# Attention's q and k loads with their rows numbered (part, d, repeat), and quad 2's load issued behind the first two shifts

## The chip, the cores and the metric

The kernel runs on one core of a Trainium2 chip. The metric is the device time of one execution in microseconds, the median of several runs. A core has five engines with a queue each: TensorE (PE, matrix products), VectorE (DVE), ScalarE (ACT), GpSimd (POOL) and SyncE (SP, which here only waits and issues DMAs), and sixteen DMA engines that all queues share.

## The reference

A block of four stages over x of shape (2, 1024, 128), each on the layer norm of x and added to it: a gated convolution mix, a feed-forward stage, attention and the feed-forward stage again. The change is in the attention, of 16 heads with 8 dimensions each:

```
qkv = x @ qkv_w.T + qkv_b
qkv = qkv.reshape(B, S, H, 3 * hd)            # B 2, S 1024, H 16, hd 8
qkv = jnp.transpose(qkv, (2, 0, 3, 1))
q, k, v = jnp.split(qkv, 3, axis=2)
scores = jnp.einsum('hbds,hbdt->hbst', q, k) / jnp.sqrt(jnp.float32(hd))
w = jax.nn.softmax(scores, axis=-1)
attn = jnp.einsum('hbst,hbdt->hbsd', w, v)
```

## The kernel before

All values of the first two stages stay in SBUF. For attention, q and k are made in four chunks of 512 tokens (NCH 4, two for each batch) for all heads at once. Each is split into three bfloat16 parts whose sum is the float32 value (PARTS 3). `store_parts(c)` (L308 to L314) writes the parts of chunk c to the DRAM tensors q_scr and k_scr, six DMAs of 128 KB for a chunk. The stored layout is (part, g and d, chunk, j, token), and the stores' access pattern has j (4) outermost.

Attention then runs over eight quads, each four heads of one batch (n = 0 to 7; b = n // 4). A quad's q and k come back from DRAM by `load_quad(n)` (L316 to L327), six DMAs: for each i of the three parts one for q and one for k. Each fills 24 rows (partitions) of the tile qt or kt with 8 KB apiece, 192 KB. Since the product of two sums of three parts has nine terms, and d has 8 values, a score is a sum over 72 rows (QK_ROWS): the rows of qt hold q's part i three times, those of kt all three parts of k against it. Three buffers for each of qt and kt take the quads in turn (NBUF 3; the third buffer lies in the memory of val, and so the trace calls it val).

Three further rows hold the shift: the negated maximum of each row of scores, in three bfloat16 parts, against rows of ones in kt. The exponent's argument thus comes out of one product over 96 rows (L1294). The maximum comes from products of its own over 72 rows (L1229), each of which VectorE reduces (L895). After the 32 units of half a quad, `turn_max` (L1236) turns the maxima, VectorE negates them (L908), GpSimd splits them into nm_s (L446 to L452), and SyncE writes them into qt by `load_shift(hn)` (L329 to L336), three DMAs of 4 KB that wait for shift_split.

TensorE's order in attention: it waits for quad 0's loads, runs 32 units of maxima for half 0 of quad 0 and 16 of half 1 (LEAD), and waits for shift 0 before the first exponent product. Then each step (16 a quad) has four exponent products (e), four maxima ahead of time (m) and the product of the previous step's exponentials with v (v), by ORDER "emememevm" (L57). The maxima of the next quad begin at step 4, with a wait for its loads (qk_in, L1308). ScalarE computes the exponentials (L648).

SyncE's order around the change stands in L338 to L361: ones into kt, the parts of chunks 0 and 1, a wait for both, load_quad(0), the parts of chunks 2 and 3, load_quad(1) and load_quad(2), load_shift(0). In the loop over n then load_quad(n + 2) for n from 1, after a wait for the exponent products that read the buffer, load_shift(2n + 1) and load_shift(2n + 2). A DMA that waits holds up all issues behind it on this queue.

Of the kernel before, what the change touches and what calls it, by code (L numbers as in the profile page):

```python
# [21 lines left out]
B, L, D = 2, 1024, 128  # L22
# [15 lines left out]
H, HD = 16, 8  # L38
QH = 4
GQ = H // QH  # L40
NQ = B * GQ
PARTS = 3
# [3 lines left out]
NBUF = 3  # L46
# [65 lines left out]
def build(nc, ins, out):  # L112
# [3 lines left out]
    with ctx:  # L116
        def sb(name, shape, dt=F32):
            return ctx.enter_context(nc.sbuf_tensor(name, shape, dt))

        def sem(name):  # L120
            return ctx.enter_context(nc.semaphore(name))
# [54 lines left out]
        h = sb("h", [P, NT, D])  # L176
# [51 lines left out]
        k_scr = nc.dram_tensor("k_scr", [PARTS, GQ * HD, NCH, QH, CH], BF16, kind="Internal").ap()  # L228
# [28 lines left out]
        qk_in = [sem(f"qk_in{r}") for r in range(NBUF)]  # L257
# [19 lines left out]
        @block.sync  # L277
        def _(sp):
            for c in range(NCH):
                sp.dma_start(x[:, TC * c:TC * c + TC, :], x_src[:, TC * c:TC * c + TC, :]).then_inc(s_x[c], 16)  # L280
            for at, v in vectors[5:]:
                sp.dma_start(vec_n[at:at + v.shape[0], :], v).then_inc(s_vec, 16)
            for at, v in q_k_biases:
                sp.dma_start(vec_n[at:at + 1, :].rearrange("a (h d) -> a h d", d=HD), v).then_inc(s_vec, 16)
            for dst, src in ((ksym[:, :, :], sym_k.rearrange("(k p) o t -> p k (o t)", p=P)),
                             (a_n[:, :, :], A_d.rearrange("(k p) s -> p k s", p=P)),
                             (kdwa[:, :, :], dwa_k.rearrange("(k p) o t -> p k (o t)", p=P))):
                sp.dma_start(dst, src).then_inc(s_w_taps, 16)
            sp.dma_start(wfc_n[:, :, :], wfc_d.rearrange("(m p) d -> p m d", p=P)).then_inc(s_w_tern, 16)
            sp.dma_start(wpr_n[:, :], wproj_d).then_inc(s_w_tern, 16)  # L290
            for dst, src in ((pw_n[:, :, :], pw_w.rearrange("(k p) c -> p k c", p=P)), (hb_n[:, :], hb_w),
                             (ha_n[:, :], ha_w), (fu_n[:, :, :], fuse_w.rearrange("(k p) c -> p k c", p=P)),
                             (ow_n[:, :], out_w), (bm_n[:, :], Bm_d)):
                sp.dma_start(dst, src).then_inc(s_w_mix, 16)
            sp.dma_start(u_n[:, :, :], u_d.rearrange("(m p) r -> p m r", p=P)).then_inc(s_w_ffn, 16)
            sp.dma_start(v_n[:, :], v_d).then_inc(s_w_ffn, 16)
            sp.dma_start(fb_n[:, :], fb_d).then_inc(s_w_ffn, 16)
            sp.dma_start(gate_n[:, :], gate_d.broadcast_to([RANK, 1])).then_inc(s_w_ffn, 16)

            sp.wait_ge(pads_ready, 5)  # L300
            for b in range(B):
                sp.wait_ge(u_read, 2 * (b + 1))
                for t in range(DC):
                    at = PAD + 1 - t
                    sp.dma_start(us[32 * t:32 * t + 32, b, at:at + L],
                                 u_rows[32 * t:32 * t + 32, b, :]).then_inc(us_in[b], 16)

            def store_parts(c):  # L308

                for w, scr in ((0, q_scr), (1, k_scr)):  # L310
                    sp.wait_ge(split_ready, 2 * c + w + 1)
                    for i in range(PARTS):
                        sp.dma_start(scr[i, :, c, :, :].rearrange("x j t -> j x t"),
                                     qk_s[c % 2][:, w, i, :]).then_inc(scr_done[c % 2], 16)  # L314

            def load_quad(n):  # L316
                b, g = divmod(n, GQ)
                rows = slice(g * HD, (g + 1) * HD)
                for i in range(PARTS):

                    at = i * PARTS * HD
                    src = q_scr[i, rows, 2 * b:2 * b + 2, :, :].rearrange("d h j t -> d (h j t)")
                    dst = qt[n % NBUF][at:at + PARTS * HD, :, :, :].rearrange("x h j t -> x (h j t)")
                    sp.dma_start(dst, src.unsqueeze(0).broadcast_to([PARTS, HD, QH * L])).then_inc(qk_in[n % NBUF], 16)
                    src = k_scr[:, rows, 2 * b:2 * b + 2, :, :].rearrange("i d h j t -> i d (h j t)")
                    dst = kt[n % NBUF][at:at + PARTS * HD, :, :, :].rearrange("x h j t -> x (h j t)")
                    sp.dma_start(dst, src).then_inc(qk_in[n % NBUF], 16)  # L327

            def load_shift(hn):  # L329

                sp.wait_ge(shift_split, hn + 1)
                n, half = divmod(hn, 2)
                for i in range(PARTS):
                    dst = qt[n % NBUF][SHIFT_ROW + i:SHIFT_ROW + i + 1, half, :, :]
                    sp.dma_start(dst.rearrange("a j (k p) -> a (j k) p", p=P),
                                 nm_s[:, i, :]).then_inc(shift_in, 16)  # L336

            sp.wait_ge(consts_ready, 2 * NBUF + 1)  # L338
            for r in range(NBUF):
                sp.dma_start(kt[r][SHIFT_ROW:SHIFT_ROW + PARTS, :, :, :].rearrange("i h j t -> i (h j t)"),  # L340
                             ones_rows).then_inc(qk_in[r], 16)
            store_parts(0)
            store_parts(1)
            for i in range(2):
                sp.wait_ge(scr_done[i], STORED)
            load_quad(0)
            store_parts(2)
            store_parts(3)
            for n in range(1, NBUF):
                load_quad(n)  # L350
            load_shift(0)
            for n in range(NQ):
                if 1 <= n and n + 2 < NQ:
                    sp.wait_ge(exp_mm, STEPS * QH * n)
                    if n + 2 == GQ:
                        for i in range(2):
                            sp.wait_ge(scr_done[i], 2 * STORED)
                    load_quad(n + 2)
                load_shift(2 * n + 1)
                if n + 1 < NQ:  # L360
                    load_shift(2 * n + 2)  # L361
            for c in range(NCH):
                sp.wait_ge(tok_read, TOK_F2[c] + 1)
                sp.dma_start(out_dst[:, TC * c:TC * c + TC, :], x[:, TC * c:TC * c + TC, :]).then_inc(stored, 16)
            sp.wait_ge(stored, 16 * NCH)
# [1009 lines left out]
```

## Time and profile before

| | us |
|---|---|
| median of 3 runs | 629.66 |
| lowest, highest | 626.11, 629.94 |
| span of the profiled execution | 623.5 |
| TensorE busy | 546.7 (88%) |
| VectorE busy | 480.4 (77%) |
| ScalarE busy | 349.4 (56%) |
| GpSimd busy | 113.0 (18%) |

The profile is of one execution. Times are from the start of its span, which is shorter than the measured time of a run. The page's chain follows the work that ended last back from the end, at each step to what released it. PE is TensorE's products and PEld its weight loads. A line such as L1229 is one of the kernel, out<-in are tiles. Idle time of an engine that is not the bottleneck costs nothing. What the DMA queues moved:

```profile
DMA packets 14664, 18.95 MB, mean 30 GB/s; under 512 B 3801, under 2 KB 12936, under 8 KB 13448
q1 hardware_dynamic: 13818, 17.54, 8.2%
```

### The profile page before, as it was taken

Reading aid. Unit: us, or ns where it says so; the run is one execution under the profiler, and the core shown is the slowest. Engines: PE = TensorE matmul, PEld = TensorE weight load, DVE = VectorE, ACT = ScalarE, POOL = GpSimd, SP = SyncE. Lnnn points to the kernel's source line nnn. Section 1 sums busy time; section 2 is a strip of 40 time slices with the busy share of each in tenths; the row PEclk is TensorE's granted clock in tenths of the full one; section 3 lists DMA queues with packets and bytes.
Section 4 is the critical chain, followed back from the end, with each engine's and each line's share of the span. In section 5 each row is a group of like instructions: output and inputs, shape, how many; then the busy total and the mean of one; then the engine's idle time right before and its main releaser. Section 6 shows DMA issues by size and latency. Waiting matters only on the chain.

```text
span 623.5 us, 9634 instructions
## 1 busy us (share of the span) xinstructions
PE 546.7 (88%) x2831; PEld 218.8 (35%) x2831; DVE 480.4 (77%) x965; ACT 349.4 (56%) x667; POOL 113.0 (18%) x155
## 2 busy tenths in 40 slices
PE   2986899872591699999999999899999999999887
PEld 2443656561110133333333333233333333323366
DVE  6999579971593388888898898788888888863473
ACT  2764314433000377777777677677777777778551
POOL 6947708334000000100100100100100000000000
PEclk9997899887555599999999999999999999999999
DMA  8030000021221000010010010010010000000001
GB/s 205 8 69 0 2 1 1 5 82 74 87 85 81 25 1 2 27 52 2 29 51 2 29 51 2 32 51 2 19 61 2 2 2 1 1 2 1 1 18 52
DMA packets 14664, 18.95 MB, mean 30 GB/s; under 512 B 3801, under 2 KB 12936, under 8 KB 13448
## 3 DMA queue, kind: packets, MB, share of 16 engines
q1 hardware_dynamic: 13818, 17.54, 8.2%
q0 software_dynamic: 240, 0.46, 0.7%
q8 instruction: 28, 0.46, 0.3%
q10 hardware_dynamic: 550, 0.27, 0.1%
q14 instruction: 28, 0.22, 0.1%
HBM read 12.75 MB, written 4.19 MB: 27 GB/s over the span
## 4 chain that ended last, share of the span: by engine, by line
PE 69%; DVE 16%; DMA 8%; ACT 3%; issue 2%; SPq 2%; POOL 0%; ACTq 0%; DVEq 0%
PE ps L1256 20%; PE ps L1229 18%; PE ps L1294 17%; PE ps L1034 5%; PE ps L1044 5%; DVE mx L895 3%; DMA qt<-nm_s 3%; DVE acc L794 3%; DMA kt<-k_scr 2%; DVE h L710 2%; DVE acc L840 1%; DMA k_scr<-gate 1%; PE ps L1243 1%; ACT gate L648 1%; DVE st L687 1%
## 5 line engine op out<-in xcount | busy, mean ns | idle before, releaser
L895 DVE TENSOR_REDUCE mx<-ps 128x1 f32<-128x512 f32 x512 | 319.5, 681 | 70.8 <-PE ps L1229 70.8
L648 ACT ACTIVATE gate<-ps 128x512 f32<-128x512 f32 x256 | 134.3, 604 | 112.2 <-PE ps L1294 112.2
L1229 PE MATMUL ps<-kt,qt 72*128 72x512 bf16 x384 | 157.7, 417 | 18.0 <-DMA kt<-k_scr 18.0
L1294 PE MATMUL ps<-qt,kt 96*128 96x512 bf16 x384 | 143.0, 386 | 21.6 <-DMA qt<-nm_s 18.2
L648 ACT ACTIVATE acc<-ps 128x512 f32<-128x512 f32 x256 | 132.3, 602 | 49.8 <-PE ps L1294 49.8
L1229 PEld LDWEIGHTS ps<-kt,qt 72*128 72x128 bf16 x384 | 38.3, 100 | 131.9 <-DVE mx L895 81.0
L1256 PE MATMUL ps<-gate,v 128*32 128x512 f32 x512 | 69.3, 611 | 0.7 <-ACT o_sb L639 0.7
L1256 PE MATMUL ps<-acc,v 128*32 128x512 f32 x512 | 68.2, 605 | 0.6 <-ACT acc L648 0.6
L446 POOL CAST nm_s<-nm 16x128 bf16<-16x128 f32 x16 | 4.6, 287 | 331.4 <-DVE nm L908 331.4
L1294 PEld LDWEIGHTS ps<-qt,kt 96*128 96x128 bf16 x384 | 37.5, 99 | 65.0 <-DMA qt<-nm_s 18.8
L1229 PE MATMUL ps<-val 72*128 72x512 bf16 x128 | 48.8, 382 | 0.0
L1294 PE MATMUL ps<-val 96*128 96x512 bf16 x128 | 48.6, 380 | 0.0
L794 DVE SCALAR_TENSOR_TENSOR acc<-val,ksym,acc 128x512 f32<-128x512 f32 (+1 forms) x40 | 38.4, 1033 | 0.0
L1044 PEld LDWEIGHTS ps<-wp_T,acc 128*128 128x128 f32 x256 | 29.5, 192 | 2.4 <-issue 1.9
L1034 PE MATMUL ps<-hT,fc_T 128*128 128x512 f32 x64 | 30.3, 618 | 0.0
L1044 PE MATMUL ps<-wp_T,acc 128*128 128x128 f32 x256 | 29.7, 275 | 0.0
L405 POOL TENSOR_TENSOR acc<-acc,attn 128x512 f32<-128x512 f32 x8 | 27.2, 3404 | 13.7 <-ACT attn L523 12.6
L602 ACT ACTIVATE gate<-ps 128x512 f32<-128x512 f32 x32 | 18.2, 596 | 17.6 <-DVE acc L840 10.7
L1229 PEld LDWEIGHTS ps<-val 72*128 72x128 bf16 x128 | 12.5, 98 | 34.6 <-DVE mx L895 23.5
L840 DVE TENSOR_TENSOR acc<-gate 128x512 f32<-128x512 f32 x32 | 21.5, 719 | 3.0 <-ACT gate L602 3.0
L1256 PEld LDWEIGHTS ps<-gate,v 128*32 128x32 f32 x512 | 10.6, 108 | 27.8 <-ACT acc L648 11.8
L1256 PEld LDWEIGHTS ps<-acc,v 128*32 128x32 f32 x512 | 10.1, 108 | 27.9 <-ACT acc L648 14.6
(181 smaller groups left out, 473.3 us busy)
## 6 DMA issues: line engine op xcount, KB each, us to landing
qt<-q_scr SPq DMA_DIRECT2D x18, 192.0 KB
kt<-k_scr SPq DMA_DIRECT2D x18, 192.0 KB
val<-q_scr SPq DMA_DIRECT2D x6, 192.0 KB
val<-k_scr SPq DMA_DIRECT2D x6, 192.0 KB
x<-in_L_attn_a_x SPq DMA_DIRECT2D x4, 256.0 KB, 4.5
us<-h SPq DMA_DIRECT2D x8, 128.0 KB, 2.4
out<-x SPq DMA_DIRECT2D x4, 256.0 KB, 2.2
q_scr<-attn SPq DMA_DIRECT2D x6, 128.0 KB
```

What stands on the lines that cost most here:

```text
L405: pool.tensor_tensor(dst, dst, tap_buf(j), ALU.add).then_inc(tap_added, 1)
L602: act.activation(relu[:, n % NR, :], bank(2 + i % 4), ACT.Relu).then_inc(wide_read, 1)
L648: act.activation(pexp[s % NPB][:, j, :], bank(exp_bank(n0, s * QH + j, last)[0]), ACT.Exp, scale=SCALE).then_inc(exp_done, 1)
L710: ins = dve.tensor_scalar(h[:, i, :], x[:, i, :], small[:, f, 2, i:i + 1], small[:, f, 3, i:i + 1], ALU.mult, ALU.add)
L794: ins = dve.scalar_tensor_tensor(out=dst, in0=src, scalar=ksym[:, k, j:j + 1], in1=dst, op0=ALU.mult, op1=ALU.add)
L840: dve.tensor_tensor(r2_buf[:, c % 2, m, :], r, r, ALU.mult).then_inc(sq_ready, 1)
L895: dve.tensor_reduce(mx[:, half, u // 2, u % 2:u % 2 + 1], bank(MBANKS[k % 4]), AX.X, ALU.max).then_inc(m_read, 1)
L1034: mm = pe.matmul(bank(2 + i % 4), w, a, start=(k == 0), stop=(k == len(pairs) - 1))
L1044: mm = pe.matmul(bank(6 + i % 2)[:, t * P:(t + 1) * P], a, w, start=(k == 0), stop=(k == len(group) - 1))
L1229: pe.matmul(bank(MBANKS[k % 4]), qt[r][0:QK_ROWS, half, j, c * P:(c + 1) * P], kt[r][0:QK_ROWS, keys, j, :], start=True, stop=True).then_i ...
L1256: mm = pe.matmul(bank(2)[VW * j:VW * (j + 1), :], v4[r][:, s % BT, j, :], pexp[s % NPB][:, j, :], start=(s % BT == 0), stop=(s % BT == BT ...
L1294: pe.matmul(bank(at_bank), keys, qt[r][:, half, j, :], start=True, stop=True).then_inc(exp_mm, 1)
```

## The change

In load_quad the repeat dimension of q's source moves from outermost to second, and so does the part dimension of k's source. Row 3d + r of a group of 24 rows holds what row 8r + d held before; q and k change alike. The destination, the 24 rows and the bytes are as they were. In SyncE's order load_quad(2) moves from ahead of load_shift(0) to behind load_shift(1).

```diff
@@ load_quad
-                    sp.dma_start(dst, src.unsqueeze(0).broadcast_to([PARTS, HD, QH * L])).then_inc(qk_in[n % NBUF], 16)
-                    src = k_scr[:, rows, 2 * b:2 * b + 2, :, :].rearrange("i d h j t -> i d (h j t)")
+                    sp.dma_start(dst, src.unsqueeze(1).broadcast_to([HD, PARTS, QH * L])).then_inc(qk_in[n % NBUF], 16)
+                    src = k_scr[:, rows, 2 * b:2 * b + 2, :, :].rearrange("i d h j t -> d i (h j t)")
                     dst = kt[n % NBUF][at:at + PARTS * HD, :, :, :].rearrange("x h j t -> x (h j t)")
                     sp.dma_start(dst, src).then_inc(qk_in[n % NBUF], 16)
@@ SyncE's order
             store_parts(3)
-            for n in range(1, NBUF):
-                load_quad(n)
+            load_quad(1)
             load_shift(0)
             for n in range(NQ):
                 if 1 <= n and n + 2 < NQ:
...
                     load_quad(n + 2)
                 load_shift(2 * n + 1)
+                if n == 0:
+                    load_quad(2)
                 if n + 1 < NQ:
                     load_shift(2 * n + 2)
```

## Rows read from the trace of the kernel before

**Rows 1.** The page: clock row of 40 slices, chain by engine and line, two groups.

```profile
PEclk9997899887555599999999999999999999999999
...
PE 69%; DVE 16%; DMA 8%; ACT 3%; issue 2%; SPq 2%; POOL 0%; ACTq 0%; DVEq 0%
PE ps L1256 20%; PE ps L1229 18%; PE ps L1294 17%; PE ps L1034 5%; PE ps L1044 5%; DVE mx L895 3%; DMA qt<-nm_s 3%; DVE acc L794 3%; DMA kt<-k_scr 2%; DVE h L710 2%; DVE acc L840 1%; DMA k_scr<-gate 1%; PE ps L1243 1%; ACT gate L648 1%; DVE st L687 1%
...
L1229 PE MATMUL ps<-kt,qt 72*128 72x512 bf16 x384 | 157.7, 417 | 18.0 <-DMA kt<-k_scr 18.0
L1294 PE MATMUL ps<-qt,kt 96*128 96x512 bf16 x384 | 143.0, 386 | 21.6 <-DMA qt<-nm_s 18.2
```

**Rows 2.** Chain of waits, 136 to 209 us: start us, us, what.

```profile
136.23 7.83 DMA k_scr<-gate
...
147.81 14.23 DMA kt<-k_scr
...
162.80 19.82 DVE mx L895 x33
...
187.59 20.74 DMA qt<-nm_s
```

**Rows 3.** Timeline of TensorE, 188 to 209 us: start us, us, what, idle time before.

```profile
187.74 2.40 PE L1229 MATMUL ps<-kt,qt 72*128 72x512 bf16 x4
208.38 0.61 PE L1294 MATMUL ps<-qt,kt 96*128 96x512 bf16 x1 [18.25 <-DMA qt<-nm_s]
```

**Rows 4.** Windows: stretch, length, busy us PE, PEld, DVE, ACT, POOL, PEclk, DMA, GB/s.

```profile
4.00:6.00 2.00, 0.00 (x0) 0.00 (x0) 1.50 (x8) 0.44 (x1) 2.00 (x4) 1.00 1.15 356
136.00:144.00 8.00, 7.31 (x28) 4.71 (x26) 2.88 (x6) 3.01 (x5) 2.14 (x2) 0.79 0.26 91
190.00:200.00 10.00, 0.14 (x1) 0.00 (x0) 1.86 (x4) 0.00 (x0) 0.00 (x0) 0.50 0.19 81
192.00:208.00 16.00, 0.00 (x0) 0.00 (x0) 0.00 (x0) 0.00 (x0) 0.00 (x0) 0.50 0.18 76
209.00:218.00 9.00, 9.00 (x25) 2.45 (x24) 5.44 (x8) 4.94 (x9) 0.00 (x0) 0.50 0.01 2
218.00:220.00 2.00, 2.00 (x10) 0.66 (x12) 1.78 (x4) 1.74 (x4) 0.00 (x0) 0.82 0.00 0
```

**Rows 5.** The tile nm_s, its sixteen shifts: from issue to landing.

```profile
DMA to landing us min/median/max: 1.7/1.8/20.7
```

**Rows 6.** Timeline of SyncE's queue: start us, us, line, operation, out<-in, count.

```profile
144.12 0.76 SPq L324 DMA_DIRECT2D qt<-q_scr  x1
...
148.53 9.87 SPq L313 DMA_DIRECT2D q_scr<-attn  x3
...
182.26 2.09 SPq L327 DMA_DIRECT2D val<-k_scr  x1
185.81 2.37 SPq L335 DMA_DIRECT2D qt<-nm_s  x3
228.55 1.77 SPq L335 DMA_DIRECT2D qt<-nm_s  x3
252.05 1.77 SPq L335 DMA_DIRECT2D qt<-nm_s  x3
```

**Rows 7.** Timelines of TensorE and VectorE ahead of the first maxima.

```profile
143.14 1.05 PE L1044 MATMUL ps<-att_T,hT 128*128 128x128 f32 x8
146.19 0.68 DVE L859 TENSOR_TENSOR us<-ps,bv_bc 128x512 f32<-128x512 f32 x1
```

**Rows 8.** Timeline of TensorE: quad 1's first maximum, and two turned maxima.

```profile
223.84 0.38 PE L1229 MATMUL ps<-kt,qt 72*128 72x512 bf16 x1
226.24 0.28 PE L1236 MATMUL ps<-ident,mx_row 128*16 128x128 f32 x1
249.74 0.28 PE L1236 MATMUL ps<-ident,mx_row 128*16 128x128 f32 x1
```

## The prediction

> **What bounds the kernel now.** I read the page first. TensorE is busy for 88% of the span, and the chain that ended last is 69% TensorE, yet 8% of it is transfers: qt<-nm_s 3%, kt<-k_scr 2%, k_scr<-gate 1% [rows 1]. The diff only touches transfers, so the question is where one of them holds up the program.
>
> The chain of waits between 136 and 209 us answers it [rows 2]. SyncE waits for the stores of the q and k parts until 144.06. Then it issues the six loads of quad 0, and the last lands 14.23 us after its issue, at 162.04. The row maxima follow on VectorE, 33 reductions in 19.82 us, then the merged row maxima are turned and negated, and GpSimd splits the first shift into three parts (nm_s). SyncE issues them from 185.81 [rows 6], and the last takes 20.74 us to land. TensorE, which has done its last early maximum at 190.14, starts the exponent products at 208.38 after 18.25 us of idle time [rows 3]. The reader is to see that this chain has only two transfers that could be shorter, and no compute engine works beside either: between 192 and 208 us every engine shows 0.00 busy [rows 4].
>
> Is either a matter of latency? The other landings of the shift say no: the median of all is 1.8 us, the longest 20.7 [rows 5]. So the 20.74 us are queueing. The issues on SyncE's queue show behind what [rows 6]: six loads of quad 0, twelve stores (parts of chunks 2 and 3), six loads of quad 1, six of quad 2, and then the shift. The windows give the rates [rows 4]. With loads alone (190 to 200 us) 81 GB/s move at a DMA share of 0.19, and 0.19 x 16 = 3.0 engines: 27 GB/s for each. With stores alone (136 to 144) it is 91 GB/s at 0.26, that is 4.2 engines. In the code the loads' source has an outermost dimension of 3 (the repeats for q, the parts for k), and the stores' source has one of 4 (j). A transfer thus runs on as many engines as its outermost dimension counts, here.
>
> Do these rates explain the times? A quad is 6 x 192 KB = 1,180 kB, at 81 GB/s 14.6 us. From first issue (144.12) to landing (162.04) are 17.9 us, so 3.4 us are issue and latency. The twelve stores are 12 x 128 KB = 1,573 kB, at 91 GB/s 17.3 us. From 162.0: 17.3 + 14.6 + 14.6 gives 208.5, and the shift landed at 187.59 + 20.74 = 208.33. The queue is understood to 0.2 us.
>
> **The change, part by part.** *Rows numbered with d outermost.* Each load keeps its 24 rows of 8 KB and its bytes; the sums over rows don't depend on their order, and q and k get the same one. The outermost dimension of the source goes from 3 to 8, which divides the destination's 24 rows too. By the reading above the load then runs on 8 engines. No row shows a transfer on eight, so I bound its rate from the two sides: 8 x 27 = 216 GB/s if each engine keeps what it has on three, and 8 x 22 = 178 GB/s if each falls to what sixteen give (356 GB/s at 4 to 6 us, /16 = 22) [rows 4]. A quad takes 5.5 or 6.6 us; I take 6.0, between the two, since eight lies between three and sixteen. Issue doesn't limit it: six loads go out in 0.72 us each [rows 6], 4.4 us. Quad 0 lands 14.6 - 6.0 = 8.6 us earlier, at 153.4. Below nothing isn't possible unless engines get fewer (a rival).
>
> Who else would hold TensorE then? Its last earlier product ends at 144.2, VectorE's last v tile at 146.9 [rows 7]. Both lie ahead of 153.4, so the maxima start 8.6 us earlier, and the whole train behind them too: the shift is ready at 177.2, issued to 179.6 (185.81 + 2.37 - 8.6), TensorE out of early maxima at 181.5.
>
> The Trainium skill has a rule against the full gain. "SBUF — State Buffer", section "Door 1: The DMA port swizzle", says that a transfer's rate depends on how many of 16 ports its partitions reach, some 27.2 GB/s each, four neighbouring partitions to a port. A 24-row load reaches 6, so by an estimate from that page 163 GB/s and 7.2 us for a quad: a gain of 7.4 us at this place instead of 8.6, and a total 1.2 us higher. No row of before can decide it, because three engines stay below six ports.
>
> *Quad 2's load behind the first two shifts.* Six issues (4.3 us of SyncE's time) and 14.6 us of queue (6.0 at the new rate) leave the place ahead of load_shift(0). Ahead of the shift now: quad 0 done by about 151.6 (landing less latency), stores 17.3 us to 168.9, quad 1 6.0 us to 174.9 on the engines that both use. That is 2.3 us before the shift is issued at 177.2. The shift then takes its usual 1.8 us after the last issue: 187.59 - 8.6 + 1.8 = 180.8, still 0.7 us before TensorE is free for it (181.5). The stall of 18.25 us becomes about nothing. If the queue needs longer, the first 3.0 us cost nothing and each further one a whole us.
>
> What is late next? Quad 2's load now waits for shift 1, which is issued at 228.55 [rows 6], in the new time 26.8 us earlier: 201.8, landing by about 212 with the new rate. Its first use is the maxima of quad 2, from step 4 of quad 1. Half a quad is 23.5 us (the turned maxima at 226.24 and 249.74), and quad 1's first maximum is at 223.84, so quad 2's is at 223.84 + 47.0 = 270.8, in the new time 244.0 [rows 8]: 32 us of cover. Queued behind the moved issues is load_shift(2), whose issue at 252.05 follows POOL's split, not the queue [rows 6]; it becomes 225, long after the six issues. GpSimd's queue isn't passed.
>
> *Later quads.* Five more loads of six transfers get shorter, but TensorE waits for transfers only at two places in the stretch, and the page shows 18.0 us for the one form and 18.2 of the other in the whole run, which are these [rows 1, 3]. Worth nothing; their cover is the exponent work of the quad before.
>
> *TensorE's clock.* It was granted half speed, 1.2 GHz, from 156 us on (the fives of the clock row, slices 11 to 14 of 15.6 us) [rows 1], in the maxima and in the stall, and went back to 2.4 GHz about 10 us after the exponent products began (0.50 at 209 to 218, 0.82 in 218 to 220) [rows 4]. I shift this stretch as it is. If the maxima ahead without an idle gap brought the rise forward, up to 5 us more would come back (about 10 us at half speed); if it came later by the same chance, 1 or 2 us would be lost. The maxima, though, ran 28 us at 0.50 with no rise, so I take nothing.
>
> **Sum.** Profiled execution: 623.5 - 8.6 - 18.2 = 596.7. The runs' median is 629.66, 6.2 above the span; the difference applies there too: 602.8. The three runs reach from 626.11 to 629.94, so the measure is good to about 2 us, and half a per cent, and 1% (6 us) is about what can be told from no change.
>
> **Rivals.**
> (a) *The rate stays.* If not the outer dimension but the 24 rows set the number of engines (24 rows are three times 8), the loads stay at 81 GB/s. For it: 3 fits 24/8. Against it: stores with 128 rows ran at 4.2 engines, which 128/8 = 16 doesn't give. Then only the move counts: the shift lands behind quad 1, 14.6 us earlier, TensorE starts at 193.8: 629.7 - 14.6 = 615.1.
> (b) *The shift still waits.* Stores and loads meet on engines 0 to 3 and stores slow down, or loads keep to 178 GB/s or the ports' rate. For it: only 3.0 us of slack. With 3 to 6 us lost: 606 to 609.
> (c) *The clock rises sooner*: 598 to 601, with the price above.
> (d) *Slower.* The new order puts a load on fewer engines. It decides from two engines down: at 54 GB/s a quad takes 21.8 us, and 144.1 + 3.4 + 21.8 + 17.3 + 21.8 = 208.4, the shift's landing of today. On one engine (27 GB/s) a quad takes 43.7 us: the shift lands at about 252, and the time is 673. Against it: both shapes seen so far ran on as many engines as they had outermost rows, and there are more now.
> The rule of the Trainium skill in "DMA: Bandwidth & Descriptors", section "Why a DMA increments its semaphore by 16 and not by 1", is that the engines are the largest number up to 16 that divides both outermost sizes; it gives 8 for 8 and 24, against (a) and (d), and the trace's 3 and 4 agree with it.
>
> **Chances.** The forecast (600 to 606) 0.72; (a) 0.09; (b) 0.11; (c) 0.06; (d) 0.02. The likeliest is the number: 602.8. The range takes the forecast, (b) and most of (c): 598.5 to 609. Faster by over 1% hold all but (d): 0.97. Within 1%: 0.01. Slower: 0.02.
>
> **What would show it.** The DMA share during quad 0's load near 0.5 instead of 0.2, and its rate near 200 GB/s; TensorE's wait for kt<-k_scr 9 us instead of 18.0; maxima starting at 153 to 155; the landing of the first shift under 3 us, with TensorE's wait for it gone; quad 2's issues at about 202 and no new wait at quad 1's step 4. I am wrong if the share stays at 0.19, if the shift still takes over 5 us to land, or if the clock's rise moves by more than 3 us against the first exponent product.

## The result, and the profile after

The changed kernel takes 601.62 us (median; 601.03 to 602.98) against 629.8 (626.11 to 630.09) for the kernel before: a ratio of 0.9588, interval 0.956 to 0.9616. The span of its profiled execution is 599.0 us, before 623.5.

First the chain of waits of the changed kernel, in the same stretch as [rows 2] (start us, us, what):

```profile
144.64 0.69 SPq L324
...
148.14 6.94 DMA kt<-k_scr
...
155.22 0.60 PE ps L1230
...
155.84 19.82 DVE mx L896 x33
...
176.19 6.96 PE ps L1230 x13
183.15 0.43 PE ps L1295
```

The six loads of quad 0 land 6.94 us after the last issue instead of 14.23. From there VectorE's 33 reductions take 19.82 us, as before. Then the chain stays on TensorE: the step "DMA qt<-nm_s", 20.74 us in [rows 2], isn't there. TensorE's timeline says the same against [rows 3], and so does the tile nm_s against [rows 5]:

```profile
175.98 7.16 PE L1230 MATMUL ps<-kt,qt 72*128 72x512 bf16 x13
182.94 0.63 PE L1295 MATMUL ps<-qt,kt 96*128 96x512 bf16 x1
```

```profile
DMA to landing us min/median/max: 1.7/1.8/2.8
```

The first exponent product carries no idle time; it starts at 182.94 instead of 208.38. The longest landing of any shift is 2.8 us, where it was 20.7; the first shift lands in 1.8. The page's groups put what is left of the waits for transfers at one place, against 18.0 and 18.2 in [rows 1]:

```profile
L1230 PE MATMUL ps<-kt,qt 72*128 72x512 bf16 x384 | 157.7, 417 | 10.6 <-DMA kt<-k_scr 10.6
L1295 PE MATMUL ps<-qt,kt 96*128 96x512 bf16 x384 | 143.1, 387 | 3.2 <-issue 2.0
```

Windows of the changed kernel (stretch, length, busy us of PE, PEld, DVE, ACT, POOL, granted clock, DMA share, GB/s), against [rows 4]:

```profile
147.00:151.00 4.00, 0.00 (x0) 0.00 (x0) 0.39 (x1) 1.74 (x2) 3.16 (x5) 0.60 0.53 172
176.00:178.00 2.00, 2.00 (x6) 0.42 (x4) 2.00 (x5) 0.00 (x0) 0.70 (x2) 0.50 0.22 78
178.00:180.00 2.00, 2.00 (x5) 0.31 (x3) 2.00 (x4) 0.00 (x0) 0.69 (x2) 0.50 0.11 41
374.00:382.00 8.00, 7.23 (x32) 1.84 (x33) 3.63 (x7) 4.62 (x9) 0.40 (x1) 0.79 0.41 134
```

During quad 0's load the DMA share is 0.53, that of eight engines and a little, and 172 GB/s move: 21.5 for each engine, where three engines had 27. Quad 1 is through only between 178 and 180 us, about when the shift is issued (178.82).

**Where 24.5 us of span come from.** The first exponent product starts 25.4 us earlier. The granted clock rose 9.2 us after it instead of 10.2, which gives half a us more. So the turned maximum of quad 0's second half is at 200.25 instead of 226.24, 26.0 earlier, and the distance stays until 343 us of the kernel before. At one turn of the loop over quads TensorE idles for 2 us in both kernels (1.98 at 374.77, before 2.07 at 400.85). In the profile of before the clock held behind it (1.00 from 400 to 408 us); in the changed kernel's it falls once, to about half speed from 376 to 380 us (0.62 and 0.53 in its two halves; 0.79 in the last window above). That costs 1.45 us: the turned maximum at 438.90 before is at 414.36, 24.5 earlier, and so is the end.

### The profile page after: what moved, and what is told of

Its sections match the earlier page's. It is cut to its first block, busy times and chain, and to the rows that moved or that the text cites. A ratio compares the mean times of both kernels' runs of the same rounds, so it can differ in the third digit from the quotient of the medians.

```text
span 599.0 us, 9634 instructions
## 1 busy us (share of the span) xinstructions
PE 548.1 (92%) x2831; PEld 218.8 (37%) x2831; DVE 479.6 (80%) x965; ACT 349.2 (58%) x667; POOL 112.2 (19%) x155
## 4 chain that ended last, share of the span: by engine, by line
PE 73%; DVE 17%; DMA 3%; ACT 3%; issue 2%; SPq 1%; POOL 0%; ACTq 0%; DVEq 0%
PE ps L1257 21%; PE ps L1230 20%; PE ps L1295 18%; PE ps L1035 6%; PE ps L1045 5%; DVE acc L795 3%; DVE mx L896 3%; DVE h L711 2%; DMA k_scr<-gate 1%; DVE acc L841 1%; PE ps L1244 1%; ACT gate L649 1%; DMA kt<-k_scr 1%; DVE st L688 1%; ACT acc L649 1%
## 5 line engine op out<-in xcount | busy, mean ns | idle before, releaser
L1230 PE MATMUL ps<-kt,qt 72*128 72x512 bf16 x384 | 157.7, 417 | 10.6 <-DMA kt<-k_scr 10.6
L603 ACT ACTIVATE gate<-ps 128x512 f32<-128x512 f32 x32 | 18.2, 597 | 17.6 <-DVE acc L841 10.7
L841 DVE TENSOR_TENSOR acc<-gate 128x512 f32<-128x512 f32 x32 | 21.5, 718 | 3.0 <-ACT gate L603 3.0
L1257 PEld LDWEIGHTS ps<-gate,v 128*32 128x32 f32 x512 | 10.5, 108 | 27.6 <-ACT acc L649 11.8
L1257 PEld LDWEIGHTS ps<-acc,v 128*32 128x32 f32 x512 | 10.1, 108 | 27.9 <-ACT acc L649 14.6
```

The source lines that it names most:

```text
L603: act.activation(relu[:, n % NR, :], bank(2 + i % 4), ACT.Relu).then_inc(wide_read, 1)
L841: dve.tensor_tensor(r2_buf[:, c % 2, m, :], r, r, ALU.mult).then_inc(sq_ready, 1)
L1230: pe.matmul(bank(MBANKS[k % 4]), qt[r][0:QK_ROWS, half, j, c * P:(c + 1) * P], kt[r][0:QK_ROWS, keys, j, :], start=True, stop=True).then_i ...
L1257: mm = pe.matmul(bank(2)[VW * j:VW * (j + 1), :], v4[r][:, s % BT, j, :], pexp[s % NPB][:, j, :], start=(s % BT == 0), stop=(s % BT == BT ...
```

## The experiments

All are variants of the two kernels. Only where said do stored layouts differ; all compute the reference's output in full. The diffs are excerpts against the changed kernel, without their indentation; "..." stands for what is left out, and where a quad has more than six loads, the semaphore counts grow with them. Several profiles issue quad 0's first load up to 1.3 us later than the changed kernel's (144.64), so times are compared from that issue where it matters.

**The move alone (order_only).** The row order is that of the kernel before:

```diff
-sp.dma_start(dst, src.unsqueeze(1).broadcast_to([HD, PARTS, QH * L]))...
-src = k_scr[:, rows, 2 * b:2 * b + 2, :, :].rearrange("i d h j t -> d i (h j t)")
+sp.dma_start(dst, src.unsqueeze(0).broadcast_to([PARTS, HD, QH * L]))...
+src = k_scr[:, rows, 2 * b:2 * b + 2, :, :].rearrange("i d h j t -> i d (h j t)")
```

> Only the move: quad 2's loads behind the first two shifts, the rows as in the kernel before. Theory (a transfer runs on as many DMA engines as its outermost dimension counts, so the two parts of the change act through one queue): quad 0 lands as before at 162, the shift stands behind the stores and quad 1 only, so it lands 14.6 us earlier, at 193.8, and TensorE's idle time before the first exponent product is 18.25 - 14.5 = 3.7 us. About 615 us, 14.5 below the kernel before. Rival (the gain comes from the new row order alone): 629 to 630.

613.09 us (ratio 0.9758, 0.9723 to 0.9792, beside runs of before at 627.62). TensorE waits 3.5 us for the shift, where 3.7 were expected, and 14.5 us are gone, as the theory had it.

**The row order alone (rows_only).** Quad 2's loads are back ahead of load_shift(0).

> Only the new row order; quad 2's loads stay ahead of the first shift. Theory: quad 0 lands at 155 as in the changed kernel. The queue ahead of the shift is then quad 0, stores 17.3, quads 1 and 2 at 7.1 each: quad 1 is through at about 177, quad 2 at 184, and the shift lands at 184 to 186 while TensorE is free for it at 183. So 1 to 3 us of the stall stay, and the run takes 603 to 605: with the faster loads the move is worth only 1 to 3 us. Rival (the move carries most of the gain whatever the rate is): the shift still stands behind a whole quad's loads and 14 us are missing, 612 or more.

610.81 us (0.973, 0.9685 to 0.9774). Between the two expectations, and nearer to the rival. Its chain:

```profile
149.05 7.17 DMA kt<-k_scr
...
181.23 11.39 DMA qt<-nm_s
...
192.67 0.61 PE ps L1294
```

Quad 0 lands 7.17 us after its last issue, nearly as in the changed kernel, but the shift lands at 192.6, not at 184 to 186, and TensorE waits 8.4 us. The windows show what was missing from my sum:

```profile
168.00:172.00 4.00, 4.00 (x7) 0.62 (x6) 4.00 (x8) 0.00 (x0) 0.00 (x0) 0.50 0.53 172
172.00:184.00 12.00, 11.33 (x22) 2.10 (x21) 12.00 (x23) 0.00 (x0) 1.40 (x4) 0.50 0.51 109
```

The share is that of eight engines in both. By the rate in [rows 4] the stores keep four engines busy until about 172 (154.4 + 17.3), while the other four have begun with quad 1 (issued from 165.88). From 172 us all eight carry loads, but they move 109 GB/s, where quad 0's loads on eight engines had 172 in the changed kernel. The first four are then behind the others: the two halves work at different loads. The changed kernel has a shorter such stretch (115 GB/s at a share of 0.48 from 172 to 174 us). Whether this is the cause is taken up with st16_q2first.

**Fewer engines (eng4, eng2).** Each load is cut into two of 4 values of d, or four of 2. A quad's rows, bytes and order are those of the changed kernel; the outermost dimension falls, each DMA fills 12 or 6 rows instead of 24, and the issues grow:

```diff
+for d0 in range(0, HD, 4):                 # eng2: 2
+    rows = slice(g * HD + d0, g * HD + d0 + 4)
+    part = slice(at + PARTS * d0, at + PARTS * (d0 + 4))
-    dst = qt[n % NBUF][at:at + PARTS * HD, :, :, :]...
+    dst = qt[n % NBUF][part, :, :, :]...
```

> The changed kernel with each load cut into two of 4 values of d (12 rows): outermost dimension 4, same rows, same bytes, same row order, twice the issues. Theory (the outermost dimension sets the engines): four engines at 24 to 27 GB/s, 96 to 108 GB/s; a quad takes 11 to 12.3 us instead of 7.1, the first maximum starts at 159 to 160.5; quad 1 is through at 144.6 + 1.6 + 11.6 + 17.3 + 11.6 = 186.7, the shift lands at about 188 where TensorE is free at 187.5; 606 to 608 us. Rival (24 rows, or the row order as such, give the rate): 601.6 plus at most 1 us for the issues.

> The same cut into four of 2 values of d (6 rows): outermost dimension 2. Theory: two engines at 27 GB/s, 54 GB/s, a quad takes 21.8 us. The first maximum starts at about 169, the shift lands at about 208.4: the time of the kernel before, 628 to 631, although quad 2's loads are out of the way. Rival (24 rows, or the row order as such, give the rate): 602 to 604.

eng4: 608.78 us (0.9715, 0.9688 to 0.9742). eng2: 660.2 us (1.0545, 1.0499 to 1.0592, beside 626.97). First eng4's window, then eng2's, during quad 0's loads:

```profile
147.00:159.00 12.00, 0.00 (x0) 0.00 (x0) 0.57 (x1) 1.91 (x2) 3.29 (x5) 0.56 0.25 90
```

```profile
147.00:160.00 13.00, 0.00 (x0) 0.00 (x0) 0.93 (x2) 2.25 (x3) 3.28 (x5) 0.50 0.13 47
```

And two waits of eng2's whole span (us in total, times, the longest):

```profile
PE ps L1298 <- DMA qt<-nm_s: 20.6, 5, 11.9
...
PE ps L1298 <- DMA val<-nm_s: 10.5, 2, 5.5
```

Shares of 0.25 and 0.13 are 4 and 2 engines. That fewer rows in a DMA did it is ruled out by the other kernels: the same 24 rows had three engines before and have eight in the changed kernel, and 8 rows have eight in sp1 below. The rival falls.

eng4 came out slightly above its 606 to 608: at 90 GB/s instead of 96 to 108 the first maximum starts at 161.06, and TensorE waits 2.1 us for the shift. For eng2 I had the shift, and so the first exponent product, at about 208.4; it starts at 211.91, after 11.85 us of idle time, 3.5 later. The rest of the 33 us that it is slower than the kernel before comes afterwards: TensorE waits seven times for a shift, 31.1 us together, and only the longest is the first shift's. The six others follow the loads of quads 2 to 7. In the kernel before, a quad's loads in the loop are issued 18.0 us ahead of a shift:

```profile
257.49 0.73 SPq L324 DMA_DIRECT2D qt<-q_scr  x1
...
275.50 1.82 SPq L335 DMA_DIRECT2D qt<-nm_s  x3
```

From first issue to landing a quad takes 17.9 us on three engines: just fast enough. On two, quad 0's maxima start 26.9 us after the first issue. The six waits in the loop are 19.2 us; some 11 more stand beside a lower clock (eng2's mean over the span is 0.907, against 0.926 in base, the kernel before measured again, and 0.945 in the changed kernel), and I haven't split them.

**k's loads on twelve engines (k12).** k_scr is stored as (g d, part, chunk, j, token), and the 24 rows are one dimension:

```diff
-src = k_scr[:, rows, 2 * b:2 * b + 2, :, :].rearrange("i d h j t -> d i (h j t)")
+src = k_scr[rows, :, 2 * b:2 * b + 2, :, :].rearrange("d i h j t -> (d i) (h j t)")
...
```

> The changed kernel, with k_scr stored as (g d, part, chunk, j, token), so that the 24 rows of a k load are one dimension of 24 and divide by 12. q's loads stay at 8. Theory E (each DMA engine has about 21 us-GB/s in these loads, 167/8 GB/s, whatever rows it writes): k's loads run on 12 engines and take 0.79 us instead of 1.18, a quad 1.2 us less, the first maximum at about 154.0 instead of 155.2, 600.4 us. Theory P (the 24 rows themselves limit a transfer to some 165 GB/s): a quad takes 7.1 us as now, 601.6 us. If 8 is the limit of engines for another reason: 601.6 as well, with a DMA share of 0.5 during the loads.

603.22 us (0.9622, 0.9569 to 0.9676), no gain; from the first issue to the first maximum its profile has 11.7 us instead of 10.6. Its window in quad 0's loads:

```profile
149.00:156.00 7.00, 0.00 (x0) 0.00 (x0) 0.00 (x0) 0.78 (x1) 2.19 (x5) 0.54 0.59 123
```

More engines are busy (0.59, that of 9.4 engines) and less is moved (123 GB/s, 13 for each). Theory E is out: an engine has no rate of its own of 21 GB/s. That it got slower neither theory had. q's loads run on eight engines and k's on twelve here, so again engines may get out of step; that this is the reason isn't shown.

**Neighbouring or spread rows (sp1, sp3).** This pair changes only which rows one DMA writes. Both cut each load into three of 8 rows, 8 engines, 64 KB. They differ only in the rows that one DMA fills:

```diff
+for a in range(PARTS):
+    part = slice(at + HD * a, at + HD * (a + 1))              # sp1: 8 neighbours
+    part = slice(at + a, at + PARTS * HD, PARTS)              # sp3: every third of 24
+    src = q_scr[i, rows, 2 * b:2 * b + 2, :, :].rearrange("d h j t -> d (h j t)")
+    dst = qt[n % NBUF][part, :, :, :].rearrange("x h j t -> x (h j t)")
+    sp.dma_start(dst, src).then_inc(qk_in[n % NBUF], 16)     # and k_scr[a, rows, ...] into kt
```

> The changed kernel with each load cut into three, one for each repeat or part: 8 rows of 8 KB, 8 engines, rows numbered as in the changed kernel, so the 8 rows of a DMA lie three apart and spread over all 24. 18 DMAs a quad instead of 6. Theory E (each engine has its own rate of some 21 GB/s with eight at work) and theory P (what limits is how many groups of four neighbouring rows a transfer writes at a time; 24 rows touch six) expect the same here: the data take 7.1 us, the 18 issues at 0.6 us take 10.8, so the issues set it, the first maximum comes 13 to 14 us after the first issue, 604 to 605 us.

> The same 18 DMAs with 8 rows of 8 KB on 8 engines, but rows numbered as in the kernel before (the repeat outermost): the 8 rows of a DMA are neighbours. Theory E: as sp3, 604 to 605 us. Theory P: eight neighbours are two groups of four, and two groups give what two engines gave (53 GB/s, 26.5 each); a quad takes about 22 us, the first maximum comes 25 us after the first issue, and the loop's loads delay its shifts too: 640 to 660 us.

> The changed kernel once more, unchanged, beside the three kernels below on one chip: 601 to 603 us, with the first maximum 10.6 us after the first issue of quad 0's loads, as before.

after2 (the changed kernel again): 601.51 us, from first issue to first maximum 10.5 us (144.56 to 155.02). sp3: 605.33 us (0.9615, 0.9563 to 0.9666), 13.7 us (145.07 to 158.80). sp1: 618.59 us (0.9824, 0.9777 to 0.9871), 19.0 us (145.96 to 164.99). A window of sp3, then one of sp1, in quad 0's loads:

```profile
149.00:156.00 7.00, 0.00 (x0) 0.00 (x0) 0.00 (x0) 0.19 (x1) 1.59 (x4) 0.50 0.34 104
```

```profile
149.00:160.00 11.00, 0.00 (x0) 0.00 (x0) 0.00 (x0) 1.12 (x1) 2.77 (x5) 0.56 0.52 69
```

And the first issue on SyncE's queue in each, sp3 first, then sp1:

```profile
145.07 0.65 SPq L326 DMA_DIRECT2D qt<-q_scr  x1
```

```profile
145.96 0.29 SPq L326 DMA_DIRECT2D qt<-q_scr  x1
```

sp3 is held by its issues, as expected: its share is 0.34, between one and the next the engines have nothing to do. sp1 has eight engines busy all the time (0.52) and moves 69 GB/s, 8.6 for each. Same number of engines, same pieces, same sources: which rows are written decides. So for 8 neighbouring rows the rows set what eight engines give, not the engines. The Trainium skill, "SBUF — State Buffer", section "Door 1: The DMA port swizzle", gives 27.2 GB/s for each port that a transfer reaches, four neighbouring rows to a port. By an estimate from that page 8 neighbours get 54 GB/s and 24 rows 163. The runs' 69 and 172 lie above both, by 28% and 5%; that DMAs behind one another reach other ports is a possible reason that no run shows.

sp1's time was in neither theory's range. 19.0 - 3.4 = 15.6 us a quad instead of 22, and the loop's shifts bear that as they did the 14.6 of before: only the first one is waited for, 1.8 us. Some 5 us more are lost at the turn of the loop where TensorE idles for 2 us: the ninth and tenth of the sixteen turned maxima lie 32.5 us apart, instead of 27.3 in the changed kernel. The granted clock is 0.50 there from 394 to 400 us, while the changed kernel has some 4 us at half speed; why it is longer is open.

**Stores on sixteen engines (st16), and with quad 2 in front (st16_q2first).** The DRAM tensors have j and (g d) as neighbours, q three times over:

```diff
-sp.dma_start(scr[i, :, c, :, :].rearrange("x j t -> j x t"), qk_s[c % 2][:, w, i, :])...
+# q_scr [PARTS, NCH, QH, GQ * HD, PARTS, CH], the part broadcast over the repeats
+dst = scr[i, c, :, :, :, :].rearrange("j x a t -> (j x) a t")
...
+# k_scr [NCH, QH, GQ * HD, PARTS, CH]
+dst = scr[c, :, :, i, :].rearrange("j x t -> (j x) t")
...
+src = q_scr[i, 2 * b:2 * b + 2, :, rows, :, :].rearrange("h j d a t -> (d a) (h j) t")
+src = k_scr[2 * b:2 * b + 2, :, rows, :, :].rearrange("h j d i t -> (d i) (h j) t")
```

> The changed kernel with both DRAM tensors laid out so that the stores' 128 rows (j, g d) are one dimension: the stores run on 16 engines instead of 4. q is stored three times over (its repeats are in DRAM), so its loads' 24 rows are one dimension too; the loads' pieces are 1 KB instead of 8. Theory: the stores of chunk 1, 8 us from the last issue to landing now, land within 3 to 4 us; quad 0 lands at about 149, 6 us earlier; the first maximum starts there, since VectorE's v tile is ready at 147; 595 to 596 us. Rival (pieces of 1 KB, or three times the q bytes, eat the gain): loads take 3 us or more longer, 599 to 603.

> The kernel st16 (stores on 16 engines, loads on 12) with quad 2's loads back ahead of the first two shifts. In rows_only the eight engines of the loads ran at 107 to 115 GB/s together, with engines 0 to 3 held by the stores and 4 to 7 ahead of them. Theory: with the stores on all engines no engine runs ahead, quads 1 and 2 load at 155 to 160 GB/s and are through by about 172, before the shift is issued at 174; no stall, within 1 us of st16 (596). Rival (two quads of loads ahead of the shift always hold it up once they are shorter than 24 rows allow): a stall of 5 us or more, 601 or more.

st16: 595.98 us (0.9482, 0.9447 to 0.9517), as expected, though the first maximum starts at 150.74 and not at 149. st16_q2first: 595.33 us (0.946, 0.9414 to 0.9507). TensorE's timeline of the second, from the first maximum to the first exponent product:

```profile
148.51 19.91 PE L1234 MATMUL ps<-kt,qt 72*128 72x512 bf16 x35 [5.31 <-DMA kt<-k_scr]
...
169.27 7.20 PE L1234 MATMUL ps<-kt,qt 72*128 72x512 bf16 x13
176.26 0.63 PE L1299 MATMUL ps<-qt,kt 96*128 96x512 bf16 x1
```

Its windows, first with the stores, then with the loads of quads 1 and 2:

```profile
148.00:152.00 4.00, 3.49 (x8) 0.85 (x8) 2.87 (x5) 0.00 (x0) 0.00 (x0) 0.54 1.08 378
...
156.00:168.00 12.00, 12.00 (x21) 2.08 (x20) 12.00 (x21) 0.00 (x0) 0.00 (x0) 0.50 0.83 169
```

The stores move at 378 GB/s. The loads of quads 1 and 2 together run at 169 GB/s through 12 us, where rows_only had 109, and no exponent product waits, though quad 2 stands ahead of the shift. So the move is worth nothing here. Two things carry that. The stores are through sooner, and the loads of quads 1 and 2 are issued from 151.59 instead of 165.88. And the slow stretch is gone, as it has to be if it comes from engines out of step. How much each carries isn't split. This kernel's loads also run on twelve engines, in pieces of 1 KB, so the stores aren't the only thing that changed, and what slows the two halves in rows_only isn't shown. By an estimate from the same section of the Trainium skill, halves that stand one group of 24 rows apart reach four or five ports together, 109 or 136 GB/s, but halves two groups apart reach six; which of these rows_only had, its trace doesn't show.

The run shows one more thing: twelve engines move hardly more into 24 rows than the 172 GB/s of eight. It is 169 GB/s here, at a share of 0.83 (twelve sixteenths are 0.75, and the sixteen engines of the stores show 1.08), and 179 from 140 to 144 us, in quad 0's loads. From eight engines on, more of them bring little there, with the piece size as another difference.

**The kernel before once more (base).**

> The kernel before once more, unchanged, for a second profile. The profiled execution of before had a span of 623.5, which is 6.2 below its runs' median; that of the changed kernel lies 2.0 below its own run (599.0 and 601.03). If the profiled execution of before was one of the short ones (626.11), a second one has a span near 627.5, and the extra 4 us stand in one place of the trace. If not, spans of 623.5 come with runs of 629.7.

Span 624.6 us in a run of 626.68; its ten runs have a median of 627.61 (625.13 to 633.42). So the first of the two expectations holds in its first half: run less span is 2.1 here, about 2 as in all kernels of this study, and the profiled execution of before was a short one. The second half doesn't: 624.6 isn't 627.5. Its clock row also has a fall at the 26th slice, as the changed kernel's has:

```profile
PEclk9997899886555599999999999899999999999999
```

It costs the same here as there: from the ninth to the tenth turned maximum this profile takes 27.4 us, the changed kernel's 27.3, and the first profile of before 25.8. All other profiles of this study take 27.2 or more, so it was the first profile of before that was out of line. The rest of the spread between runs of the kernel before, some 4 us, isn't explained.

## Why the prediction was right, and where its numbers weren't

**The two stalls.** Right. Both terms acted where they were placed. The move alone gives 14.5 us, by the queue that was read from the trace and as rival (a) put it. The rows alone leave 8.4 us of the stall, more than the same queue gives, since it had no term for engines out of step.

**Eight engines.** Right: the share is 0.53, and with eng4 and eng2 the outermost dimension is shown as the cause. One reading was wrong in its wording: the 4 (j) of the stores is the outermost dimension of their DRAM destination, and their source has 128 rows. So the smaller of the two sides counted there, which the rule of the two sides that the prediction quotes covers and "the source's outermost dimension" doesn't. Rivals (a) and (d) are out for the change itself. But (d)'s point of balance was mis-sized: it counted only the first shift. At two engines the kernel is 33 us slower, since the loop's shifts wait too. "Worth nothing; their cover is the exponent work of the quad before" held for more engines, but was silent on the shift behind each quad's loads.

**The rate.** The term that was mis-sized. I took 6.0 us for a quad, from rates of three and sixteen engines. From first issue to landing are 10.4 us instead of 17.9: 7.5 gained, not 8.6, so a quad takes 7.1 us, outside both of my bounds (5.5 and 6.6), and the first maximum starts at 155.22, just past the 153 to 155 that I had named. The estimate from the Trainium skill's page was 7.2. The step that failed is that the rate of eight engines lies between those of three and sixteen: neither row said which rows were written. sp1 shows that the rows can set the rate at eight engines, and st16_q2first that 24 rows take hardly more from twelve (169 and 179 GB/s). The miss itself is small, though: 21.5 GB/s for each engine against 22 at sixteen. That the rows, and not the engines, hold the changed kernel at 172 fits these two runs but isn't shown by itself.

**The queue ahead of the shift.** The sum had quad 1 through at 174.9; it was at 178 to 180. 1.6 us of that are quad 0's later start and landing, which move the shift too (issued at 178.82 instead of 177.2); for the rest the engines out of step slow quad 1 down, to 115 GB/s. It didn't cost anything, as the first shift still landed in 1.8 us: the slack took it, and that was close. rows_only shows what the same effect costs without slack, 8.4 us. Rival (b) was therefore nearer than its chance says, and that the missing price did no harm was partly luck.

**The clock.** Half a us of gain at the rise, and 1.45 us lost at one fall in the loop, which isn't tied to the change (the kernel before has it in its second profile). The prediction read the fall to half speed off the page's slices, as "from 156 us on"; a window of before has 0.51 already from 147 to 149 us, 3 us after TensorE's last product. No term hung on it.

**The sum.** Forecast for the span 596.7, measured 599.0. Of the 2.3 us, 1.1 are from the rate, 0.5 from quad 0's first load, issued at 144.64 instead of 144.12, and 1.45 from the fall, less the half at the rise; that leaves 0.2 the other way. The forecast for the runs, 602.8, still came within 1.2 us of 601.62, and this was luck, an error the other way. "6.2 above the span; the difference applies there too" was wrong: a run is 2.0 above its span (601.03 and 599.0), and the other 4 us were the short execution that happened to be profiled. The move of the medians, 28.2 us, is larger than the 24.5 between the spans for that reason.

**What is late next.** Right. Quad 2's loads are issued from 204.72 (201.8 forecast) and no wait appears at step 4 of quad 1. Next on the path are quad 0's loads and the stores ahead of them, and st16 takes 5.6 us from there.

## What to carry to other kernels

When a small DMA takes ten times its usual landing, read its queue: bytes ahead of it over the measured rate gave the landing in the kernel before to 0.2 us. Shortening the queue and reordering it each took a part of the 18.25 us of stall (to 8.4 and to 3.5), and the two together all of it, so their gains don't add up in full. Divide a transfer's DMA share by a sixteenth to see how many engines it has, and look at the outermost dimensions of both sides if there are fewer than sixteen. Then look at which rows it writes: 8 engines moved 69 GB/s into 8 neighbouring rows and 172 into 24, and 12 engines hardly more than that (169 and 179). And where transfers on different numbers of engines follow each other in one queue, look for a stretch whose rate is low for its share; rows_only and k12 have one, with its cause open.

## What the runs showed of the hardware that I had not expected

- Eight engines move 172 GB/s into 24 rows and 69 into 8 neighbouring ones, at the same share (0.53 and 0.52).
- Behind stores that held four of the eight engines, the loads ran at 109 GB/s instead of 172 (rows_only), and with 12 engines for k and 8 for q at 123 (k12).
- Twelve engines move 169 to 179 GB/s into 24 rows, in pieces of 1 KB (st16_q2first), hardly more than eight do in pieces of 8 KB.
- A DMA to 8 neighbouring rows is issued in 0.29 us (sp1), to 8 rows three apart in 0.60 (sp3, most of them); to 24 rows on 8 engines in 0.64 (the changed kernel), on 12 in 0.39 to 0.46 (st16, k12).
